# Two-layer attention block on one core: other filler products in the head, and an earlier place for the norm's root and scale

## What is computed

```
h = group_norm(x) * gain + offset          # 32 groups of 2 channels
q, k, v = h Wq + bq, h Wk + bk, h Wv + bv  # per position
weights = softmax(q k^T / 8)               # 1024 x 1024 per image
x = x + (weights v) Wo + bo
```

## Time and profile before

| what | value |
|---|---|
| median of 3 runs | 203.67 us (203.59 to 203.68) |
| the profiled execution | 202.73 us, of which its span (first to last instruction) 200.7 us |
| PE busy | 185.6 us (92%) |
| POOL busy | 145.0 us (72%) |
| DVE busy | 140.3 us (70%) |
| ACT busy | 104.5 us (52%) |
| POOL additions L242 | 51 of 2.4 us |
| PE filler passes L588 | 142 |

### The profile page before, as it was taken

The page is one execution under the profiler, slowest core; times in us unless marked ns, Lnnn a source line. Parts: engine busy times, 40 slices in busy tenths (PEclk is TensorE's granted clock), DMA queues, the critical chain, the costliest instruction groups (busy, mean ns, idle before and its releaser), DMA issues.

```text
span 200.7 us, 3244 instructions
## 1 busy us (share of the span) xinstructions
PE 185.6 (92%) x1222; PEld 97.3 (48%) x1222; DVE 140.3 (70%) x222; ACT 104.5 (52%) x147; POOL 145.0 (72%) x84
## 2 busy tenths in 40 slices
PE   8799869999999979997999979997999999999990
PEld 7557744553644445542544445542544534554420
DVE  1779975575986479673986489673985559906965
ACT  2578157535854364655754464655754544456601
POOL 1445057699599969999599969999599959998000
PEclk9999999999999999999999999999999999999998
DMA  5334200300040003100040003100041000010101
GB/s 169 133 67 93 53 5 18 86 2 3 0 105 1 3 0 69 38 4 0 0 105 4 0 0 77 31 2 2 0 105 56 0 0 0 4 52 0 52 0 52
DMA packets 4398, 6.98 MB, mean 35 GB/s; under 512 B 736, under 2 KB 1440, under 8 KB 4384
## 3 DMA queue, kind: packets, MB, share of 16 engines
q1 hardware_dynamic: 3728, 6.06, 12.2%
q10 hardware_dynamic: 656, 0.73, 1.1%
HBM read 1.51 MB, written 1.05 MB: 13 GB/s over the span
## 4 chain that ended last, share of the span: by engine, by line
PE 35%; POOL 35%; DVE 12%; issue 8%; DMA 4%; ACT 4%; POOLq 0%; SPq 0%; DVEq 0%
POOL prob_sum L242 29%; PE ps_attn L655 9%; DVE neg_part L468 5%; PE ps_max L615 4%; PE ps_scores L635 4%; PE ps_scores L637 3%; PE ps_scores L639 3%; POOL attn L248 3%; ACT probs L330 3%; POOL xs L251 3%; PE ps_scores L643 2%; PE ps_attn L588 2%; DMA keys<-keys 2%; DMA xs<-x_dram 2%; DVE rden L572 2%
## 5 line engine op out<-in xcount | busy, mean ns | idle before, releaser
L242 POOL TENSOR_TENSOR prob_sum<-prob_sum,probs 128x1024 f32<-128x1024 f32 x43 | 102.8, 2390 | 20.3 <-ACT probs L330 16.2
L468 DVE TENSOR_REDUCE neg_part<-ps_max 128x2 f32<-128x1024 f32 x59 | 71.8, 1216 | 27.3 <-PE ps_max L616 27.3
L330 ACT ACTIVATE probs<-ps_scores 128x1024 f32<-128x1024 f32 x64 | 62.5, 1025 | 51.8 <-PE ps_scores L644 46.6
L655 PE MATMUL ps_attn<-probs,vals 128*64 128x512 f32 x256 | 61.8, 604 | 0.0
L615 PE MATMUL ps_max<-keys,q_hi 64*128 64x512 f32 x59 | 27.6, 468 | 6.8 <-DVE neg_part L468 6.1
L484 DVE RECIPROCAL rden<-den 128x128 f32<-128x128 f32 x28 | 25.1, 925 | 7.0 <-ACT den L336 7.0
L655 PEld LDWEIGHTS ps_attn<-probs,vals 128*64 128x64 f32 x256 | 15.8, 136 | 27.7 <-issue 21.4
L616 PE MATMUL ps_max<-keys,q_hi 64*128 64x512 f32 x59 | 27.7, 470 | 0.0
L635 PE MATMUL ps_scores<-q_hi,keys 64*128 64x512 f32 x64 | 25.5, 399 | 0.0
L615 PEld LDWEIGHTS ps_max<-keys,q_hi 64*128 64x128 f32 x59 | 10.8, 183 | 30.3 <-DVE neg_part L468 22.8
L636 PE MATMUL ps_scores<-q_hi,keys 64*128 64x512 f32 x64 | 25.5, 398 | 0.0
(11 more groups left out here) (90 smaller groups left out, 289.6 us busy)
## 6 DMA issues: line engine op xcount, KB each, us to landing
keys<-keys SPq DMA_DIRECT2D x32, 128.0 KB, 2.3
xs<-x_dram SPq DMA_DIRECT2D x3, 256.0 KB, 5.2
out_dram<-xs SPq DMA_DIRECT2D x3, 256.0 KB, 2.0
layer<-layers_dram ACTq DMA_DIRECT2D x2, 194.5 KB, 4.7
xs<-x_dram SPq DMA_DIRECT2D x1, 128.0 KB, 3.0
xs<-x_dram ACTq DMA_DIRECT2D x1, 128.0 KB, 3.5
q_row<-max_rows SPq DMA_DIRECT2D x8, 4.0 KB
out_dram<-xs SPq DMA_DIRECT2D x1, 128.0 KB, 1.7
```

The lines of the kernel that those rows point to most:

```text
L242: pool.tensor_tensor(prob_sum[u % 2][:, :], first[:, :], probs[t][:, :], ALU.add).then_inc(added, 1)
L330: act.activation(probs[t][:, :], ps_scores[t % 2][:, :], ACT.Exp, scale=SCALE).then_inc(exp_done, 1)
L468: dve.tensor_reduce(neg_part[u % 2][:, at:at + JS + 1:JS], ps[:, :].rearrange("p (h n) -> p h n", h=2), AX.X, ALU.max, negate=True).then_i ...
L655: mm = pe.matmul(ps_attn[half * C:(half + 1) * C, :], v, probs[t][:, cols], start=(t == 0), stop=(t == TILES - 1))
```

## The change

1. Fillers: `keep_warm` uses `ones_r` (128 x 128, fp32r) instead of `ones` (128 x 64, fp32), and writes 128 x 128. The counts change from 20, 12, 5, 4, 6 (three times), 12 to 40, 30, 13, 10, 15 (three times), 30. In passes: 142 before, 168 after. `ones_r` is set first on POOL, so that PE can start on it.
2. Image 0 is loaded by one DMA of 256 KB on SP; ACT's queue begins with the parameters.
3. POOL: the root of a unit moves ahead of the last addition of the window before (`root(w + 3)` ahead of `add(w, 7)`, instead of `root(w + 2)` ahead of `add(w, 1)`). Roots 3 to 7 move, root 2 stays.
4. DVE: in windows 1 to 5 `gn_affine(w + 2)` comes behind `row_max(w + 1, 3)` instead of ahead of it.

```diff
@@ block.sync
-            sp.dma_start(xs[0:C, slot(0)], x[0, 0:C]).then_inc(x_in[0], 16)
-            for b in range(1, B):
+            for b in range(B):
                 sp.dma_start(xs[:, slot(b)], x[b]).then_inc(x_in[b], 16)
@@ block.gpsimd
+            pool.memset(ones_r[:, :].bitcast(F32), 1.0).then_inc(ones_r_set, 1)
             pool.memset(ones[:, :], 1.0).then_inc(ones_set, 1)
...
+            root(2)
             for w in range(UNITS):
-                if w + 2 < UNITS:
-                    root(w + 2)
                 for t in range(1, TILES if w < LAST else EARLY):
                     if t == 4 and 0 < w < LAST - 1:
                         finish(w - 1)
+                    if t == TILES - 1 and w + 3 < UNITS:
+                        root(w + 3)
                     add(w, t)
@@ block.scalar
-            act.dma_start(xs[C:P, slot(0)], x[0, C:P]).then_inc(x_in[0], 16)
@@ block.vector
-            dve.wait_ge(x_in[0], 32)
+            dve.wait_ge(x_in[0], 16)
...
-                if prep:
+                if prep and not w:
                     gn_affine(w + 2)
                 if nxt:
                     row_max(w + 1, 3)
+                if prep and w:
+                    gn_affine(w + 2)
                 if nxt:
                     row_max(w + 1, 4)
@@ block.tensor
-                    pe.matmul(ps[0:C, 0:C], ones[:, :], ones[:, :], start=True, stop=True)
+                    pe.matmul(ps[:, 0:P], ones_r[:, :], ones_r[:, :], start=True, stop=True)
...
-            pe.wait_ge(ones_set, 1)
-            keep_warm(20)
+            pe.wait_ge(ones_r_set, 1)
+            keep_warm(40)
             setup(0)
-            keep_warm(12)
+            keep_warm(30)
             project(0)
-            keep_warm(5)
+            keep_warm(13)
...
-            keep_warm(4, ps_attn)
+            keep_warm(10, ps_attn)
...
-                keep_warm(6, ps_attn)
+                keep_warm(15, ps_attn)
...
-            keep_warm(12, ps_attn)
+            keep_warm(30, ps_attn)
```

More of the change, by code:

```diff
@@ L226, in _ @@
                 pool.memset(wvo[n][:, :], 0.0).then_inc(wvo_zero, 1)
-            pool.memset(ones_r[:, :].bitcast(F32), 1.0).then_inc(ones_r_set, 1)
             def root(u):
@@ L723, in _ @@
             pe.wait_ge(setup_done, 2)
-            keep_warm(12, ps_attn)
-            pe.wait_ge(ones_r_set, 1)
+            keep_warm(30, ps_attn)
+            pe.wait_ge(ones_set, 1)
             pe.wait_ge(full_done, 4)
```

## The result

The change makes the kernel slower: 223.95 us (221.34 to 225.37) against 203.68 (203.59 to 203.97), a ratio of 1.095 (1.086 to 1.104). The forecast was 207.8 us with a range of 201.5 to 210.0. The direction was right, and so was the pace of the fillers at full clock. The size was not: a second effect, the larger part of the loss, had no term in the sum.

The account below looks back on a forecast made before the run. The prediction took POOL's chain to bind the windows, with PE 1.1 us of room. To the profiled 202.73 us it added 6.6 for fillers, subtracted 2.5 for windows, and corrected to the median: 207.8 us, range 201.5 to 210.0.

Parts of the forecast that it names:

- The pace of 0.112 us, load-bound: Fillers on PE: each new pass takes 0.112 us, set by its load of 128 columns, whatever the stream costs.
- sum of +6.6 us for the head: Head, fillers gap by gap: the new ones add 6.6 us in all, between 5.5 and 7.5.
- the first gap, "+0.1": Fillers ahead of setup(0), 20 to 40 products: at 0.10 to 0.112 us a pass they add 0.1 us.
- Rival 3: First 40 passes: PE is slow there, load doubled to 0.22 us, filler time added before project(0); 210.2 us, chance 0.08.
- The windows: -2.5 forecast: Turns into windows 1 to 5: the order edits on POOL and DVE save 2.5 us, between 4.3 and 1.2.
- The cycle of 21.92: Turns into windows 2 to 5: a window lasts 21.92 us instead of 22.50, 0.6 us less each.
- Both edits belong together: Windows: POOL's root move and DVE's gain and shift move were taken as one joint step, 0.6 us a window.
- the floor by PE: Windows: a window less PE's 1.03 us of idle time, 21.47 us, is the least that PE allows.
- The root has no stall on POOL: POOL, moved root: var_eps is written by 66.65 and POOL free at 67.7, so no stall, 1.0 us to spare.
- The DMA at nothing: First image's load in one DMA: between -0.3 and +1.0 us, taken as 0.
- the filler's cover: Head: the filler holds project(0) until 9.45, 1.1 us after h was ready, which hides a later DMA.
- Rival 1: Fillers run at the stream's pace, 0.058 us a pass; 202.4 us, at the best gain of the windows 200.6; chance 0.20.

Follow-up runs that it names:

- e7: Changed kernel with only its first block of fillers in the old form (20 products of fp32, 64 columns); 208.09 us, ratio 1.023.
- e6: Changed kernel with fillers of 128 x 128 in fp32 (same weight load, twice the stream) at half the counts; 210.11 us, ratio 1.033.
- e2: Kernel before with only the root's move on POOL and the move of gain and shift on DVE; 200.34 us, ratio 0.985.
- e9: Kernel before with only gain and shift moved behind row maximum 3 on DVE, root left in place; 199.00 us, ratio 0.975.
- e3: Kernel before with only the first image loaded by one DMA on SP; 203.57 us, ratio 0.996.
- e5: Changed kernel with its fillers cut to 64 weight columns, same type, rows, streamed columns and counts; 200.47 us, ratio 0.986.
- e8: Changed kernel with fillers of 128 weight and 512 streamed columns in fp32r, counts 10, 6, 2, 2, 3, 6; 200.22 us, ratio 0.982.
- e12: Kernel before with gain and shift moved, root left, fillers of 128 x 512 in fp32r and six more in window 0; 197.62 us, ratio 0.975.
- e1: Kernel before with only the new fillers and counts, ones_r set first; 227.33 us, ratio 1.121.
- e11: Changed kernel with its own fillers but half as many (20, 13, 6, 5, 8, 15); 206.09 us, ratio 1.013.
- e10: Kernel before with only the root moved ahead of the last addition, DVE's order left; 200.22 us, ratio 0.980.
- e4: Changed kernel with the old fillers and counts, all else as changed; 200.50 us, ratio 0.985.

## Why the prediction was right in direction and wrong in size

- **The pace of 0.112 us, load-bound: right.** e7 and e6 show it at the upper level. Its sum of +6.6 us for the head stands as well: in e7 `scores(0, 0)` starts at 32.1, 8.2 later than before, and 1.6 of these are the last block's 5.14 us, where the second block, with as many passes, takes 3.56. The blocks before it hold back 3.5, 1.6, 1.3 and 1.8 us, forecast 3.45, 1.54, 1.21 and 1.77. With the clock up early the forecast of 207.8 us would have been near: e7 takes 208.09, though with those 1.6 us in it and windows that gave more than forecast.
- **The step that failed is the first gap, "+0.1".** I took the first 40 passes at 0.10 to 0.112, from the mean of the old ones. It was 0.22, and `setup(0)` came 4.4 us later, not 0.1. The row of 40 old passes in 4.10 us mixes a lower and an upper level: the first 33 of them start 0.107 us apart, the last seven 0.058. At the lower level the load of 128 columns sets a pace of 0.213. Rival 3 had that, with a chance of 0.08, but ended it after 4.1 us.
- **What was missing altogether is that the clock would stay down.** I priced the filler only as something that delays, not as what it is there for. So the blocks of 30, 13 and 10 passes held the next product back by 6.6, 3.0 and 2.3 us where 3.45, 1.54 and 1.21 were forecast, the last one by 5.4 instead of 3.45; only the three of 15, at the upper level, came out as forecast (1.82 against 1.77). The real products of the head ran at half speed too, until 33.3 us. The head took 23.6 us more, against 6.6 forecast, and the 17 us between are the clock: the difference between e6 and the changed kernel is 14, and some 2 more are in e6's own first block.
- **The windows: -2.5 forecast.** The cycle of 21.92 was 21.74, so a turn gave 0.76 instead of 0.6; the root delays the addition by 0.52 (93.48 to 94.00) and not 0.57, and the stretch of additions and `finish` is 0.13 shorter. e2 has -3.1 by the lowest times. The new wait, for the last addition that the root delays, is where it was expected. "Both edits belong together" was wrong: either alone takes the old wait away, and the DVE edit alone avoids the new one too (e9, 21.38, where the floor by PE was put at 21.47).
- **The root has no stall on POOL: right for the turns that count.** No root from 93.48 us on has idle time ahead of it; the one at 71.47, at the turn into window 1, has 0.22 us.
- **The DMA at nothing: right**, and not because of the filler's cover alone: e3, with short fillers, shows none of the up to 1.0 us either.
- **Rival 1 (0.058, the stream's pace)** fell. The branch in the Trainium skill, "TensorE: Matmul & The Clock Gate", section "Weight-path perf modes", of a faster load for 128 columns that aren't FP32 doesn't show here: 0.112 at 128 rows in fp32r. Its other half, no gain for four-byte data, fits. The section "LDWEIGHTS (loading the stationary operand)" of the same page of the Trainium skill gives columns / 1.2 in ns, an estimate of 107 for 128 columns. The trace agrees at the upper level (0.112 us); at the lower one it shows 0.213.

## What to carry to other kernels

A filler product is there to keep PE's clock up, and the profile shows whether it does: compare its pace, and that of the real products behind it, with a stretch at full clock, as the clock column reads 1.00 until the trace's first record of the clock. The fillers that did it early here were those whose stream lasts at least as long as their weight load (e5, e6, e8); ten of 128 x 512 columns did it by 5.5 us in e8 and by 11.0 in e12, where 40 of 128 x 128 failed. No run leaves the fillers out, so what they are worth in all is not shown. Where one engine waits for a small result at the head of a long queue, moving the reader back can do the same as moving the producer forward, without delaying what the producer's engine does next.

## What the runs showed of the hardware

- A weight load of 128 columns in fp32r sets a pace of 0.112 us at the upper clock level (e7) and of 0.213 at the lower (the first 40 passes of the changed kernel in 8.80 us). With 64 weight columns and 128 streamed ones it is 0.06 (e5: 30 in 2.01 us) and 0.107 (the first 33 of e5's 40 passes, which together take 4.14).
- A pass in fp32 streams about twice as long as one in fp32r: at the lower level 0.91 us against 0.43 from start to start, for 512 columns (`project(0)` and `scores(0, 0)` of the changed kernel).
- With fillers whose load lasts about twice as long as their stream (0.112 us against at most 0.058) the clock came up at 33.3 us in the changed kernel, 31.6 in e1 and 21.5 with half as many of them (e11), each time while PE ran no fillers. With the old form, with 64 weight columns, or with a stream as long as the load it came up between 4.4 and 11.0 us. For kernels with the same first block this point differs: 4.4 (before), 5.2 (e10), 5.6 (e9), 9.8 (e2), 10.3 (e4).
- Once up, the clock stayed up over load-bound blocks of 30, 13, 10 and 15 passes with real products between them (e7). It fell in a block of 30 behind 0.5 us of idle time (the changed kernel at 43.5 us, e1 at 41.8, e7 at 28.8), and not in one of 15 behind the same idle time (e11).
- The clock fell for 3.4 us in window 0 in several kernels (e4: 0.85 and 0.72 in two stretches of 4 us), after PE had idled there twice for DVE, 0.5 and 1.3 us; in other profiles with the same idle times it did not (before, e5, e9). With fillers in that idle time it read 1.00 throughout (e12). That the fillers are the reason rests on one profile and on a mean clock of 0.994 to 1.00 in all six executions.
